# Rotating the pairs of two cross attentions elementwise, over two feature chunks

## The reference, cut to what matters

```python
# layer 0: neighbours are a pair            # layer 1: the two halves of a head are a pair
x1, x2 = x[..., ::2], x[..., 1::2]          x1, x2 = x[..., :half], x[..., half:]
x1p = x1 * cos - x2 * sin
x2p = x1 * sin + x2 * cos
att = q @ k.T / 4                            # layer 0: masked by token masks; layer 1: window of 128 back
y = softmax(att) @ v
```

## Time and profile before

| | us |
|---|---|
| three runs | 2996.15, 2999.45, 3002.4 |
| profiled execution | 3001.85 |
| its span, first to last instruction | 3000.0 |
| cross0, by its first and the next stage's first instruction | 265.5 to 849.5 |
| cross1, by the same | 2194.5 to 2631.3 |

### The profile page before, as it was taken

One profiled execution on the slowest core, in us unless ns is written; L12 is line 12 of the kernel. 1 busy time (PEld: TensorE's weight loads), 2 busy tenths in 40 slices (PEclk: granted clock), 3 DMA queues, 4 the chain that ended last, 5 costly groups with the idle time before them and its releaser, 6 DMA issues. The chain is left out here.

```text
span 3000.0 us, 49276 instructions
## 1 busy us (share of the span) xinstructions
PE 2735.5 (91%) x16077; PEld 1618.7 (54%) x16093; DVE 1936.2 (65%) x4005; ACT 1450.3 (48%) x2231; POOL 1105.3 (37%) x853
## 2 busy tenths in 40 slices
PE   7997899999958899999999999999879999867998
PEld 4774333333325555555555555555445555456997
DVE  4775676766758766666575757575646666474555
ACT  2343566666668743434343434343426655443333
POOL 3233323222036343434343434343534333053333
PEclk9999899999989999999999999999989999958999
DMA  5002222222111000000000000000033332146665
GB/s 160 0 0 70 56 55 59 55 58 56 34 57 43 1 1 1 0 0 0 0 0 0 0 0 0 0 0 0 1 101 75 83 74 74 38 116 234 216 217 194
DMA packets 103205, 159.60 MB, mean 53 GB/s; under 512 B 28365, under 2 KB 63576, under 8 KB 97560
## 3 DMA queue, kind: packets, MB, share of 16 engines
q1 hardware_dynamic: 98056, 147.75, 17.2%
q0 software_dynamic: 3408, 8.46, 0.8%
q10 hardware_dynamic: 1600, 1.61, 0.2%
HBM read 91.66 MB, written 14.96 MB: 36 GB/s over the span
## 5 line engine op out<-in xcount | busy, mean ns | idle before, releaser
L1681 DVE TENSOR_REDUCE self_nmax<-self_SM 128x2 f32<-128x1024 f32 x256 | 314.0, 1226 | 184.4 <-PE self_SM L1578 177.7
L523 DVE TENSOR_REDUCE cross_nmax<-cross_S 128x2 f32<-128x1024 f32 x256 | 311.9, 1224 | 150.3 <-PE cross_S L348 149.4
L1659 ACT ACTIVATE self_PT<-self_ST 128x1024 f32<-128x1024 f32 x256 | 262.5, 1025 | 291.9 <-PE self_ST L1601 291.9
L1719 POOL TENSOR_TENSOR self_U<-self_PT 128x1024 f32<-128x1024 f32 x64 | 153.1, 2393 | 622.2 <-ACT self_PT L1659 622.2
L1722 POOL TENSOR_TENSOR self_U<-self_U,self_PT 128x1024 f32<-128x1024 f32 x128 | 304.0, 2375 | 55.4 <-ACT self_PT L1659 50.9
L457 ACT ACTIVATE cross_PT<-cross_S 128x1024 f32<-128x1024 f32 x256 | 260.9, 1026 | 116.4 <-PE cross_S L359 115.5
L1193 DVE CUSTOM_DVE_ANT_0 cross_banded<-cross_S,cross_outside 128x256 f32<-128x256 f32 (+1 forms) x512 | 169.8, 388 | 117.3 <-PE cross_S L985 116.4
L1611 PE MATMUL self_OP<-self_PT,self_V 128*64 128x512 f32 x1024 | 233.8, 598 | 10.1 <-ACT self_PT L1659 10.1
L1695 DVE RECIPROCAL self_rcp<-self_W 128x512 f32<-128x512 f32 x64 | 214.1, 3346 | 8.4 <-PE self_W L1618 8.4
L1113 ACT ACTIVATE cross_PT<-cross_S 128x1024 f32<-128x1024 f32 x128 | 131.1, 1025 | 97.9 <-PE cross_S L1001 95.7
L1611 PEld LDWEIGHTS self_OP<-self_PT,self_V 128*64 128x64 f32 x1024 | 69.5, 136 | 139.2 <-issue 132.8
(11 more groups left out here) (437 smaller groups left out, 6407.6 us busy)
## 6 DMA issues: line engine op xcount, KB each, us to landing
moe_staged<-in_L_ffn_W SPq DMA_DIRECT2D x36, 1024.0 KB
cross_ks<-cross_parts SPq DMA_DIRECT2D x384, 64.0 KB, 2.3
cross_qs<-cross_parts SPq DMA_DIRECT2D x376, 64.0 KB, 2.3
all_x<-in_L_ffn_W SPq DMA_DIRECT2D x14, 1024.0 KB
all_x<-sorted_rows SPq DMA_DIRECT2D x83, 130.0 KB, 2.1
cross_cT<-in_ctx_T SPq DMA_DIRECT2D x16, 512.0 KB, 5.2
sorted_rows<-all_spare_row SPq DMA_DIRECT2D x1, 5460.0 KB, 23.8
all_x<-in_x SPq DMA_DIRECT2D x8, 512.0 KB, 3.8
```

Source lines behind the costliest of these rows:

```text
L523: dve.tensor_reduce(nmax[:, g % 2, 0:R, n % PER_G], S[:, slot[st], :, :], AX.X, ALU.max, negate=True).then_inc(s_maxed, 1)
L1659: act.activation(PT[:, k, :, :], ST[:, :, :], ACT.Exp).then_inc(exped.sem, 1)
L1681: dve.tensor_reduce(nmax[:, i, 0:P:D], SM[:, :, :], AX.X, ALU.max, negate=True).then_inc(maxed.sem, 1)
L1719: pool.tensor_tensor(U[:, c % 2, :, :], PT[:, 0, :, :], PT[:, 1, :, :], ALU.add).then_inc(added.sem, 1)
```

## The change

In both stages the order of the features is changed on the host, in the columns of the weights of q and k, so that the first element of every pair lies in chunk 0 and the second, at the same partition, in chunk 1. `rows` gets four buffers (q and k, two chunks each), `parts` keeps its size but is indexed by q or k, high or remainder, chunk. The turn is then elementwise between the two chunks: two sine products on VectorE (step `sine`, now from SBUF), and on GpSimd two cosine products, a subtraction and an addition (step `rope`); the remainder becomes a step of its own (`low`). turnm and its matmul are gone. In the first batch VectorE does q's turn and remainder; its sine products lie in the last buffer of PT.

The stacks use rows 0 to 47 of each half as before, but a feature of the pair at 8 * d + 2 * j + chunk: every eighth partition over all 128. One DMA then covers both halves, for one chunk. The rows in between are zero; VectorE clears ks and GpSimd clears qs at the start of a stage, and the score matmuls have 62 and 64 rows instead of 48 to 51. In cross0 the mask of the queries is folded into the layer norm's scale (`keep`) instead of a product on GpSimd. Mask rows and maxima take two DMAs a group where they took four.

The due times of most preparation steps are moved.

```diff
-    QK_ORDER = (1, 0, 3, 2)
+    HALF, STEP = 64, 8
+    MASK_ROW, QROWS, MROWS = 6, 62, 64
...
-        for n, t in zip(QK_ORDER, (-44.0, -36.0, -28.0, -20.0)):
-            for part in range(KC):
-                at[("qk", b, n, part)] = o + t + part + 0.5
-            at[("rot", b, n)] = o + t + 2.9
-            at[("rope", b, n)] = o + t + 3.0
-            at[("high", b, n)] = o + t + 5.6
+        for w, t in ((1, -36.5), (0, -28.5)):
+            for e in range(2):
+                for part in range(KC):
+                    at[("qk", b, 2 * e + w, part)] = o + t + 2 * e + part
+        for w, t in ((1, -34.9), (0, -26.9)):
+            for e in range(2):
+                at[("sine", b, 2 * e + w)] = o + t + 2.0 * e
+            at[("rope", b, w)] = o + t + 2.2
+        for w, t in ((1, -28.0), (0, -20.9)):
+            for e in range(2):
+                at[("high", b, 2 * e + w)] = o + t + 0.1 * e
+            at[("low", b, w)] = o + t + 0.3
         for g in range(GROUPS):
-            free = o + PER_G * g - 23.8
-            for s4 in range(4):
-                at[("stack", b, g, s4)] = free + 0.8 * s4
+            free = PER_G * g - 23.8
+            at[("stack", b, g, 1)] = o + max(free, -25.6 + 0.2 * g)
+            at[("stack", b, g, 0)] = o + max(free + 0.8, -18.2 + 0.2 * g)
...
-        for m, ts in enumerate(((-14.4, -12.8), (1.6, 3.2))):
+        for m, ts in enumerate(((-20.5, -19.5), (-18.5, -17.5))):
...
-        for m, ts in enumerate(((41.6, 42.0), (43.2, 43.25))):
+        for m, ts in enumerate(((51.5, 52.5), (53.5, 54.5))):
...
+            pair, from_ = slice(2 * g, 2 * g + 2), slice(32 * g, 32 * g + 32)
+            for j, part in enumerate((0, 0, 1) if which else (0, 1, 0)):
+                if part not in parts_of:
+                    continue
+                for e in range(2):
+                    eng.dma_start(stack[2 * j + e::STEP, pair, :].bitcast(F32), parts[from_, which, part, e, :].bitcast(F32)).then_inc(sem, 16)
...
-                    roped(act, b, n, 1)
-                    if b:
-                        for g in (n // 2 * 2, n // 2 * 2 + 1):
+                    turned(act, b, w)
+                    if b and e == 0:
+                        for g in range(GROUPS):
                             stacked(act, b - 1, g)
-                    act.copy(parts[:, n, 0, :], rows[:, n % 2, :]).then_inc(s_high, 1)
+                    act.copy(parts[:, w, 0, e, :], rows[:, w, e, :]).then_inc(s_high, 1)
...
-                    dve.tensor_tensor(rsin[:, n % 2, :], src, sin[:, :], ALU.mult).then_inc(s_dve, 1)
+                    dve.tensor_tensor(sine_of(b, w)[:, e, :], rows[:, w, e, :], sin[:, :], ALU.mult).then_inc(s_sine, 1)
...
+            pool.memset(qs[:, :, :].bitcast(F32), 0.0).then_inc(s_zero, 1)
...
+                elif kind == "rope":
+                    base = TURN * (nth_rope[st] - 1)
+                    for e in range(2):
+                        pool.wait_ge(s_sine, nth_sine[("sine", b, 2 * e + n)])
+                        pool.tensor_tensor(rows[:, n, e, :], rows[:, n, e, :], cos[:, :], ALU.mult).then_inc(s_rope, 1)
+                    for e, op in enumerate((ALU.subtract, ALU.add)):
+                        pool.wait_ge(s_rope, base + 1 + e)
+                        pool.tensor_tensor(rows[:, n, e, :], rows[:, n, e, :], rsin[:, 1 - e, :], op).then_inc(s_rope, 1)
```

and in cross1, with the same edits otherwise:

```diff
-        for n, t in zip(QK_ORDER, (-24.0, -20.0, -16.0, -12.0)):
-            for part in range(KC):
-                at[("qk", b, n, part)] = o + t + part + 0.5
-            at[("rot", b, n)] = o + t + 2.5
-            at[("rope", b, n)] = o + t + 3.0
-            at[("high", b, n)] = o + t + 5.0
+        for n, ts in ((1, (-22.5, -21.5)), (3, (-20.7, -19.7)), (0, (-18.6, -17.8)), (2, (-17.2, -16.4))):
+            for part, t in enumerate(ts):
+                at[("qk", b, n, part)] = o + t
+        for w, t in ((1, -20.9), (0, -16.9)):
+            at[("sine", b, w)] = o + t
+            at[("sine", b, 2 + w)] = o + t + (1.7 if w else 0.9)
+            at[("rope", b, w)] = o + t + (1.8 if w else 1.0)
+        for w, t in ((1, -14.8), (0, -13.2)):
+            for e in range(2):
+                at[("high", b, 2 * e + w)] = o + t + 0.05 * e
+            at[("low", b, w)] = o + t + 0.3
```

More of the change, by code:

```diff
@@ L145, in spread_attention @@
             at[("back", b, c)] = o + t
-        for m, ts in enumerate(((41.6, 42.0), (43.2, 43.25))):
+        for m, ts in enumerate(((51.5, 52.5), (53.5, 54.5))):
             for part, t in enumerate(ts):
                 at[("out", b, m, part)] = o + t
[L150 to L157, removed]
+    start = {("root", 0, 0): -31.5, ("htok", 0, 0): -31.1, ("root", 1, 0): -31.0, ("htok", 1, 0): -27.5,
+             ("init", 0, 0): -31.4, ("cast", 0, 0): -30.9,
+             ("sine", 0, 1): -30.2, ("sine", 0, 3): -29.9, ("rope", 0, 1): -29.7, ("sine", 0, 0): -29.5, ("sine", 0, 2): -29.3, ("rope", 0, 0): -29.0,
+             ("low", 0, 1): -28.7, ("high", 0, 1): -28.8, ("high", 0, 3): -28.75, ("high", 0, 0): -28.3, ("high", 0, 2): -28.25}
     for i in range(NT):
@@ L160, in spread_attention @@
         start[("stat", 1, i)] = -31.2 + 0.05 * i
-    for n, t in ((1, -30.0), (0, -29.8), (3, -28.8), (2, -28.0)):
+    for n, t in ((1, -31.0), (3, -30.5), (0, -30.0), (2, -29.8)):
         for part in range(KC):
             start[("qk", 0, n, part)] = t + 0.1 * part
+    for c in range(KC):
+        start[("norm", 0, c)] = -30.75 + 0.1 * c
     for m, t in enumerate((-29.2, -28.5)):
@@ L178, in finishing @@
         return [st for st in steps if st[0] not in last_part or st[3] == last_part[st[0]]]
-    RINGED = ("norm", "qk", "rot", "v", "turn", "back", "out", "mt")
+    RINGED = ("norm", "qk", "v", "turn", "back", "out", "mt")
     BY_ACT = ("norm", "qk", "v", "back", "value")
-    ACT_DMA = [("stack", 0, 0, 3), ("mdma", 0, 0)]
+    ACT_DMA = [("stack", 0, 0, 2), ("mdma", 0, 0)]
     pe_steps = in_order(RINGED + ("max", "exact", "value"))
@@ L258, in spread_attention @@
         PT = s.sb("PT", [P, PTS, R, T])
+        first_sin = PT[:, PTS - 1, :, :]
         V = s.sb("V", [P, 2, NT, H, 2 * D])
@@ L428, in pe_program @@
                         m.then_inc(s_full, 1)
-                elif kind == "rot":
-                    dst = free_bank(st)
-                    pe.wait_ge(s_act, nth_act[("qk", b, n, KC - 1)])
-                    if b == 0:
-                        pe.wait_ge(s_rot, 48)
-                    pe.matmul(dst, turnm[:, :], rows[:, n % 2, :], start=True, stop=True).then_inc(s_full, 1)
                 elif kind == "v":
@@ L564, in dve_program @@
[L564 to L570 removed]
+                    dve.wait_ge(s_sine, nth_sine[("sine", b, 2)])
@@ L796, in finishing @@
         return [st for st in steps if st[0] not in last_part or st[3] == last_part[st[0]]]
-    RINGED = ("norm", "qk", "rot", "v", "turn", "back", "out", "mt", "fix")
+    RINGED = ("norm", "qk", "v", "turn", "back", "out", "mt", "fix")
     BY_ACT = ("norm", "qk", "v", "back", "value")
-    ACT_DMA = [("stack", 0, 0, 3), ("mdma", 0, 0)]
+    ACT_DMA = [("stack", 0, 0, 2), ("mdma", 0, 0)]
     pe_steps = in_order(RINGED + ("cover", "max", "exact", "value"))
@@ L1242, in dve_program @@
-                    dve.tensor_tensor(row, low.bitcast(F32), rsin[:, n % 2, :], ALU.add).then_inc(s_early, 1)
-                    dve.wait_ge(s_early, 2)
-                    dve.wait_ge(s_high, nth_high[("high", b, n)])
-                    dve.wait_ge(s_early, ROPE - 1)
-                    dve.tensor_tensor(low, row, parts[:, n, 0, :].bitcast(F32), ALU.subtract).then_inc(s_early, 1)
+                    dve.wait_ge(s_sine, nth_sine[("sine", b, 2)])
+                    for e in range(2):
+                        dve.tensor_tensor(rows[:, 0, e, :], rows[:, 0, e, :], cos[:, :], ALU.mult).then_inc(s_early, 1)
@@ new lines, in dve_program @@
+                    for e, op in enumerate((ALU.subtract, ALU.add)):
+                        dve.wait_ge(s_early, e + 1)
+                        dve.tensor_tensor(rows[:, 0, e, :], rows[:, 0, e, :], first_sin[:, 1 - e, :], op).then_inc(s_early, 1)
+                    for e in range(2):
+                        dve.wait_ge(s_high, nth_high[("high", b, 2 * e)])
+                        dve.wait_ge(s_early, 3 + e)
+                        dve.tensor_tensor(parts[:, 0, 1, e, :], rows[:, 0, e, :], parts[:, 0, 0, e, :].bitcast(F32), ALU.subtract).then_inc(s_early, 1)
```

490 lines of the change are left out of this document (223 added, 267 removed).

## The result

The changed kernel takes 2978.72 us (median of four runs, 2978.18 to 2979.29) against 2999.53 (four runs): ratio 0.9931, 95% interval 0.9918 to 0.9943. It is faster by 20.8 us (0.7%) where 49 were forecast; inside the range of 2905 to 2990, outside the forecast's own 2930 to 2970.

| | before | after | forecast | measured |
|---|---|---|---|---|
| cross0 | 584.0 | 535.6 | -36 | -48.3 |
| feed-forward and self attention (not touched) | 1345.0 | 1351.8 | 0 | +6.8 |
| cross1 | 436.8 | 454.3 | -13 | +17.5 |

A forecast was written before the change was run, and what follows sets the result against it. The prediction took TensorE's written order to bound cross0 and cross1. Cross0 -36 and cross1 -13 summed to -49 us, from a profiled 3001.85 to 2953 and a median of 2950 us; range 2905 to 2990, the forecast's own 2930 to 2970.

The forecast's parts named there:

- so the two casts behind it cost 0.6 more: 2.1. Batch: -3.9 + 2.1 = -1.8.: Cross1 batch: freed slots give 3.9 us; ScalarE's 1.5 us stack wait plus 0.6 for casts takes back 2.1.
- The freed slots: TensorE without turn matmuls: four turns a batch, 4.8 us freed in cross0 and 3.9 in cross1.
- full clock granted in both windows: TensorE in cross0 and cross1: full clock read in the windows of before; no term for losing it.
- 0, bounds -4 and +5: Cross1 start: root later, next batch's eight projection steps precede the first exact score; no net change in us.
- Cross0's batch, -4.4: Cross0 batch 4.4 us shorter, taken between -3.5 by differences and -4.7 by a count from starts.
- The list: Cross0 batch by differences: 7.1 us freed, less 2.6 wait and 1.0 for layer-norm copies, -3.5.
- the 1.0 behind the layer norm's copies: Cross0 batch: the layer norm's four ScalarE copies (2.07 us, at unit 16) cost 1.0 us.
- the wait of 2.6: Cross0 batch: k's rounding copy on ScalarE waits 2.6 us for the previous batch's whole stack, passed through to TensorE.
- The count anew from starts: Cross0 batch summed from TensorE start-to-start slots: 59.4 us, with the two waits 63.0, which is -4.7.
- Cross0's start, -4: Cross0 start 4 us shorter, bounds -9 and +4: first maximum at about 295, maxima lead to about 312.
- Dear DMAs: Rival, chance 0.08: strided stack DMAs cost more to issue, SP bounds cross1 above 0.85 us apiece; about 3063 us.
- Hidden wait: Rival, chance 0.22: the new stack wait is hidden in both stages, only freed time counts, 82 us; 2917 us.

The follow-up runs named there:

- c1_both: Changed kernel with two cross1 edits, layer-norm copies due 2.1 units later and own semaphores for k's stack DMAs: 2946.2 us, ratio 0.984.
- c1_fill: Changed kernel with unused TensorE products added where TensorE stood in cross1's batches: 2970.7 us, ratio 0.991.
- c0_turn: Changed kernel with four unused turn-sized products given back to TensorE per cross0 batch (batches 1 to 7): 2994.3 us, ratio 0.999.
- c1_both_pad: c1_both plus 28 unused one-column products issued while TensorE waits ahead of cross0's first maximum: 2935.2 us, ratio 0.979.
- best3: best2 with only group 0's q stack still due later, and GpSimd's clear back ahead of cross1's first root: 2926.9 us, ratio 0.977.
- c1_htok: Changed kernel with cross1's four layer-norm copies due 2.1 units later (o - 26.9 for o - 29.0): 2965.9 us, ratio 0.990.
- c1_ksem: Changed kernel with own semaphores for k's stack DMAs in cross1, so k's first cast waits for k's rows alone: 2964.5 us, ratio 0.989.
- best2: c1_both_pad with layer-norm copies as own steps in both stages, and cross1's clear, root and all q stacks later: 2952.4 us, ratio 0.985.

## Why the prediction was right or wrong

**Where it failed: "so the two casts behind it cost 0.6 more: 2.1. Batch: -3.9 + 2.1 = -1.8."** The freed slots were right: without its idle time TensorE took 49.2 us of a batch before and takes 45.4 in c1_both (four batches at full clock), 3.8 less for 3.9. The wait was right too: 1.34 us here, 1.3 to 2.2 in five other batches and 3.1 in one, for 1.5. What was queued behind the waiting instruction was not followed far enough. The layer norm's copies stand at o - 29, that is unit 3 of the running batch, right behind q's casts, which the change moves to -13.2; the prediction counted these copies in cross0 alone. TensorE stood 4.6 us in the batch shown (1.37 + 3.22) in place of 2.1, and then the clock fell, for which the prediction had no term at all: it took "full clock granted in both windows" as given. The parts close. A batch went from 49.2 to 54.0 us, the mean of the second to the sixth: 3.8 less by the slots and 5.5 more by TensorE's idle time, where there was next to none, which leaves 3.1 for the clock; c1_fill gave 2.7 of them back by the clock alone. So cross1's batch grew, which the prediction had named as a sign of being wrong. Seven batches came to +24.8 us for -13.

**Cross1's ends.** Start "0, bounds -4 and +5": +3.2, from the stage's start to its first exp. The end was taken as unchanged and gave 10.5: in the kernel before, q's stack of the last batch came late, twice (TensorE's timeline, before):

```profile
2579.08 0.50 PE L985 MATMUL cross_S<-cross_ks,cross_qs 48*128 48x128 f32 x4 [1.23 <-DMA cross_qs<-cross_parts]
...
2590.61 0.80 PE L985 MATMUL cross_S<-cross_ks,cross_qs 48*128 48x128 f32 x4 [3.00 <-DMA cross_qs<-cross_parts]
```

with the clock of that batch at 0.84. After, no score of it waits for a stack and the clock is 1.00. No experiment took this apart.

**The untouched stages, taken as fixed,** grew by 6.8 us, with 128 instruction packets for 76; c0_turn and c1_both_pad show that the amount of code ahead decides.

**Cross0's batch, -4.4: -5.2, right in its slots, wrong in its waits.** TensorE's busy time fell by 4.6 us a batch for 4.8. The list had 2.3 us of stalls go and 3.6 come, 1.3 more; TensorE's idle time went from 3.0 to 2.4 us. Of what was to come, the 1.0 behind the layer norm's copies was 0.7 (it is gone in best3, where the copies are steps of their own), and the wait of 2.6 was 0.28 in the batch below and at most 1.0 in others. The landing was timed rightly: SP's last issue of the group, and the cast, in the timelines after, with the last exact score T0 at 494.65:

```profile
503.29 0.55 SPq L335 DMA_DIRECT2D cross_qs<-cross_qmask  x1
```

```profile
505.23 1.14 ACT L512 CAST cross_parts<-cross_rows 128x512 fp32r<-128x512 f32 x2 [0.28 <-DMA cross_qs<-cross_qmask]
```

10.6 us after T0, for 10.7. But ScalarE came free at 504.95, 10.3 after it, not 8.1: a due time of -28.0 ties with unit 4's exp, which goes first, so five intervals lie ahead of the cast. The count anew from starts held better than the list of differences: 59.4 us without waits, and TensorE is busy 60.1. That the count with its waits, 63.0, lies so near 62.5 owes something to luck: it holds 3.6 us of waits, and TensorE idles 2.4, half of it for copies and maxima to which the count gave no wait. Of the stage's other 12 us of gain some 5 are its first batch, where the clock was at 0.90 and is at 1.00 (windows before, then after), and 4 to 5 lie between the last batch's first exp and the stage's end (64.3 us before, 58.8 after). No experiment took these apart.

```profile
316.80:382.61 65.81, 59.75 (x306) 21.51 (x304) 46.62 (x56) 42.23 (x55) 19.88 (x19) 0.90 0.19 47
...
315.62:372.07 56.45, 52.95 (x306) 20.25 (x304) 47.09 (x56) 42.65 (x56) 16.84 (x17) 1.00 0.25 64
```

**Cross0's start, -4: -1.8,** from the stage's start (265.5 before, 266.0 after) to the first exact score. First maximum at 297.28 for 295, first exact score at 315.09 for 312 (TensorE, after):

```profile
297.28 0.79 PE L374 MATMUL cross_S<-cross_ks,cross_qs 62*128 62x512 f32 x2 [9.17 <-DMA cross_qs<-cross_parts]
...
315.09 0.50 PE L385 MATMUL cross_S<-cross_qs,cross_ks 64*128 64x512 f32 x2
```

GpSimd's cosine product alone, VectorE's sine product alone, and then q's addition and subtraction on VectorE beside k's remainder on GpSimd, two products each:

```profile
279.01 1.26 POOL L632 TENSOR_TENSOR cross_rows<-cross_rows,cross_cos 128x512 f32<-128x512 f32 x1
...
281.96 0.69 DVE L576 TENSOR_TENSOR cross_rsin<-cross_rows,cross_sin 128x512 f32<-128x512 f32 x1 [3.98 <-ACT cross_rows L505]
...
288.15 3.15 POOL L640 TENSOR_TENSOR cross_parts<-cross_rows,cross_parts 128x512 fp32r<-128x512 f32 x2 [0.79 <-ACT cross_parts L512]
...
288.43 3.42 DVE L583 TENSOR_TENSOR cross_rows<-cross_rows,cross_PT 128x512 f32<-128x512 f32 x2
```

1.7 us each on VectorE and 1.5 to 1.7 on GpSimd side by side, where one alone takes 0.69 and 1.26. So the slowdown that the prediction weighed is there, and costs VectorE 1.0 us a product instead of 0.6.

**The rivals.** Dear DMAs: refuted, six issues take 3.73 us after (0.62 each). Hidden wait: nearly true of cross0, not of cross1; the strided rows land in 2.0 us for 2.3, sooner by what that rival had estimated. "TensorE was not alone the bound" came nearest in time (2982), but not as told: no engine was full; one engine had a pile in two units, and the clock made it dear.

## What to carry to other kernels

When a wait lands on an in-order engine, list everything that the engine does until its next delivery to the bottleneck, from all batches that are in flight, not only what the diff moves. A bottleneck engine that was always fed has its clock to lose: price a new stall of a few microseconds at its length, and allow for a slow stretch behind it as well, here 3 to 4 us a batch. And a stage that no line touches can still move when code ahead of it grows or shrinks, so compare stage by stage before looking for a cause inside the change.

## What had not been expected of the hardware

A granted clock that hung on 1 us: 1.39 + 1.28 us of standing left it at 1.00, 2.35 + 1.28 brought it to 0.50 for some 10 us (c1_htok). In c1_ksem one stall of 3.12 to 3.14 us a batch put four batches at 0.93 and one at 0.97, and in best2 stalls of 3.25 us and more left most batches at 0.97, so length alone does not decide it; what else does stays open. Useless matmuls made a stage 14 us shorter. And 28 one-column products, run while TensorE waited anyway, took 11 us off stages hundreds of microseconds later.
